# Gated cross-attention block on one core: inputs as one wide array, full-width fillers, rings of four, a new order

## The reference

```python
q  = layernorm(x);   qp = (q @ W1.T + b1) @ W2.T + b2;   kp = (ctx @ W1.T + b1) @ W2.T + b2
x  = x + tanh(g_xattn) * softmax(qp @ kp.T / sqrt(128) + mask) @ ctx
h  = relu(fixed_quant(quant(layernorm(x)) @ quant(w1).T + quant(b1)))      # 512 hidden features
x  = x + tanh(g_ffn) * (quant(h) @ quant(w2).T + quant(b2))
```

## Time and profile before

| what | value |
|---|---|
| runs of the kernel | 67.88, 69.7, 67.76 us |
| median | 67.88 us |
| profiled execution, span from first to last instruction | 68.7 us |
| the profiled execution's own time | not listed apart; its span lies 0.8 us above the median |
| busy: PE, DVE, ACT, POOL | 61.4, 54.9, 50.4, 48.1 us |
| instructions | 1887 |
| read from and written to memory | 6.75 MB, 2.10 MB |

### The profile page before, as it was taken

One profiled execution on the slowest core, in us unless ns is written; L12 is line 12 of the kernel. 1 busy time (PEld: TensorE's weight loads), 2 busy tenths in 40 slices (PEclk: granted clock), 3 DMA queues, 4 the chain that ended last, 5 costly groups with the idle time before them and its releaser, 6 DMA issues.

```text
span 68.7 us, 1887 instructions
## 1 busy us (share of the span) xinstructions
PE 61.4 (89%) x557; PEld 47.7 (69%) x557; DVE 54.9 (80%) x304; ACT 50.4 (73%) x137; POOL 48.1 (70%) x100
## 2 busy tenths in 40 slices
PE   4959999998999799898989999999999999998740
PEld 4939965783587559385956968897979778464520
DVE  4554814769819899999999999999999999896530
ACT  0710442898947966896999989999989979679610
POOL 5939075399995799967989999988999308770000
PEclk9999999999999999999999999999999999999999
DMA  0899999999999991000000002000304041242142
GB/s 0 243 280 337 261 381 266 310 252 294 310 225 297 248 206 36 0 14 0 5 0 5 0 2 74 10 0 20 132 0 153 16 152 47 106 153 100 53 157 76
DMA packets 5547, 8.96 MB, mean 131 GB/s; under 512 B 744, under 2 KB 2777, under 8 KB 5537
## 3 DMA queue, kind: packets, MB, share of 16 engines
q1 hardware_dynamic: 5247, 8.66, 42.8%
q10 hardware_dynamic: 290, 0.19, 0.9%
HBM read 6.75 MB, written 2.10 MB: 129 GB/s over the span
## 4 chain that ended last, share of the span: by engine, by line
PE 54%; DVE 17%; ACT 14%; DMA 5%; issue 5%; ACTq 1%; DVEq 0%
PE bank_A L460 9%; PE bank_T L422 8%; PE bank_S L444 8%; PE bank_O L501 7%; ACT pr L568 6%; DVE x_sb L671 5%; DMA ap_sb<-in_attn_par 5%; PE bank_H L486 5%; ACT h L595 4%; PE bank_H L388 4%; PE bank_A L453 4%; DVE st L612 3%; PE bank_T L435 3%; DVE h L698 3%; DVE y_sb L707 2%
## 5 line engine op out<-in xcount | busy, mean ns | idle before, releaser
L595 ACT ACTIVATE h<-bank_H,fb_q 128x512 int8<-128x512 f32 (+1 forms) x27 | 15.8, 642 | 2.3 <-PE bank_H L486 2.2
L612 DVE BATCH_NORM_STATS2 st<-x_sb 128x6 f32<-128x128 f32 x64 | 14.0, 277 | 1.4 <-DMA x_sb<-in_x 1.3
L356 POOL TENSOR_SCALAR xq<-x_sb,nm,rs 128x128 int8<-128x128 f32 x30 | 13.2, 458 | 0.5
L568 ACT ACTIVATE pr<-sc,mn 128x120 f32<-128x120 f32 x32 | 12.2, 384 | 1.8 <-DVE mn L659 1.8
L334 POOL TENSOR_TENSOR rs<-ve,half 128x4 f32<-128x4 f32 (+1 forms) x9 | 8.5, 945 | 7.0 <-DVE nm L619 7.0
L346 POOL TENSOR_SCALAR xn<-x_sb,nm,rs 128x128 f32<-128x128 f32 x28 | 12.3, 453 | 0.6
L338 POOL TENSOR_TENSOR rs<-ve,half 128x4 f32<-128x4 f32 (+1 forms) x9 | 8.5, 941 | 4.3 <-DVE nm L619 4.3
L659 DVE CUSTOM_DVE_ANT_0 sc<-bank_S,mask_neg 128x120 f32<-128x120 f32 x32 | 7.1, 273 | 3.9 <-PE bank_S L444 3.9
L671 DVE SCALAR_TENSOR_TENSOR x_sb<-bank_A,rec,x_sb 128x128 f32<-128x128 f32 x32 | 9.1, 341 | 1.1 <-DVE rec L664 0.9
L444 PE MATMUL bank_S<-kpT,xaT 128*128 128x120 f32 x64 | 9.4, 290 | 0.3 <-DVE mn L659 0.3
L444 PEld LDWEIGHTS bank_S<-kpT,xaT 128*128 128x128 f32 x64 | 8.4, 200 | 1.8 <-issue 1.5
(11 more groups left out here) (78 smaller groups left out, 99.2 us busy)
## 6 DMA issues: line engine op xcount, KB each, us to landing
x_sb<-in_x SPq DMA_DIRECT2D x7, 256.0 KB, 8.1
out_y<-y_sb SPq DMA_DIRECT2D x7, 256.0 KB, 2.0
kT_sb<-in_ctx_kT SPq DMA_DIRECT2D x7, 240.0 KB, 8.5
v_sb<-in_ctx_v SPq DMA_DIRECT2D x7, 240.0 KB, 9.5
mp_sb<-in_mlp_par SPq DMA_DIRECT2D x1, 514.0 KB, 6.5
x_sb<-in_x SPq DMA_DIRECT2D x2, 128.0 KB, 8.2
out_y<-y_sb SPq DMA_DIRECT2D x2, 128.0 KB, 1.7
kT_sb<-in_ctx_kT SPq DMA_DIRECT2D x2, 120.0 KB, 8.3
```

Source lines behind the costliest of these rows:

```text
L356: nc.gpsimd.tensor_scalar(low_byte(xq16[g % RING], tile(j)), x_sb[:, of(g, j)], nm2[:, of(g, j, 1)], rs2[:, of(g, j, 1)], ALU.add, ALU.mul ...
L568: nc.scalar.activation(pr[i][:, j, :], sc[i][:, j, :], ACT.Exp, scale=-1.0, bias=mn[:, of(g, j, 1)], accum_out=den[:, of(g, j, 1)]).then_i ...
L595: nc.scalar.activation(low_byte(h16[g % RING], hcols(c, g)), bank_H[c][:, cols(g)], ACT.Relu, bias=fb1_q[:, c:c + 1]).then_inc(h_act[c], 1)
L612: nc.vector.bn_stats(st[:, START[g] + j, :], x_sb[:, of(g, j)]).then_inc(st_done, 1)
```

## The change

All inputs but the row of gates lie in one array of 128 rows, "feed", whose columns stand in the order in which they are loaded; values (v) are padded from 120 to 128 rows. LOADS names fourteen transfers on SP and ACT's one ("a", the attention parameters): x0; k0 with the mask; x1; v0 with k1; x2 with v1; the weights "w"; then k(g), x(g+1), v(g) of a group as one transfer of 752 KB, k7 x8 v7 of 624 KB, and k8 v8. Each transfer has one semaphore, for which every reader of any of its parts waits. ACT no longer loads the mask.

Fillers are 128 columns wide instead of 64: 30 at the start, 12 after the first fold matmul, 3 before project_keys(0); the other packs are gone. RING is 4; one more of the large byte memsets runs on DVE (HBYTES_DVE = 2), as does the fourth xq16 one, and POOL keeps two. DUE now holds places in each engine's own order; who does which tile or chunk is as before, while the order differs on every engine. The core of the diff; the new places stand in full for the steps that the text speaks of:

```diff
-RING = 3
-
-
+RING = 4
 XN_ON_POOL = [2, 3, 4, 4, 4, 4, 3, 2, 2]
 XQ_ON_POOL = [2, 3, 4, 4, 4, 4, 4, 4, 1]
 RELU_ON_ACT = [3, 4, 3, 3, 2, 3, 3, 3, 3]
-
-
+HBYTES_DVE = 2
+LOADS = ['a', 'x0', 'k0 m', 'x1', 'v0 k1', 'x2 v1', 'w', 'k2 x3 v2', 'k3 x4 v3', 'k4 x5 v4', 'k5 x6 v5', 'k6 x7 v6',
+ 'k7 x8 v7', 'k8 v8']
+ACT_LOADS = [0]
+OPENING = 30
+FILLERS = [12, 3]
...
+    fold_mm1=[1],
+    fold_mm2=[2],
+    transpose_x=[3, 8, 14, 18, 24, 30, 41, 48, 61],
+    spread_gates=[4],
+    project_keys=[5, 6, 11, 15, 20, 27, 34, 44, 58],
+    scores=[7, 10, 17, 21, 28, 37, 45, 52, 63],
+    transpose_probs=[9, 16, 23, 29, 35, 43, 51, 57, 67],
+    attend=[12, 19, 26, 32, 38, 46, 54, 60, 69],
+    fold_base=[13],
+    transpose_xq=[22, 33, 39, 47, 53, 59, 64, 70, 73],
+    hidden=[25, 36, 42, 50, 56, 62, 66, 72, 75],
+    mlp_out=[31, 40, 49, 55, 65, 68, 71, 74, 76],
+    copy_xT=[1, 8, 12, 16, 22, 29, 40, 48, 60],
+    copy_keys=[2, 5, 11, 14, 19, 26, 32, 44, 58],
+    exponentials=[7, 13, 17, 25, 30, 39, 47, 54, 65],
+    copy_probsT=[9, 15, 21, 28, 33, 42, 50, 56, 68],
+    scale_weights=[10],
+    copy_xqT=[20, 31, 38, 46, 53, 57, 63, 70, 74],
+    stats1=[1, 3, 5, 9, 13, 15, 18, 33, 38],
+    fold_cp1=[2],
+    fold_cp2=[4],
+    row_maxima=[6, 10, 16, 19, 26, 34, 42, 48, 57],
+    normalise_dve=[0, 7, 0, 0, 0, 0, 30, 40, 0],
+    reciprocals=[8, 14, 20, 25, 32, 39, 47, 52, 61],
+    residual=[11, 17, 22, 28, 35, 43, 49, 55, 63],
+    stats2=[12, 21, 24, 31, 37, 45, 51, 58, 64],
+    relu_dve3=[23, 0, 41, 46, 53, 56, 60, 67, 69],
+    quantise_dve=[0, 27, 0, 0, 0, 0, 0, 0, 66],
+    result=[29, 36, 44, 50, 59, 62, 65, 68, 70],
+    rstd1=[1, 3, 5, 8, 11, 13, 19, 23, 29],
+    normalise_pool=[2, 4, 6, 9, 14, 16, 22, 26, 31],
+    widen_weights=[7],
+    rstd2=[10, 17, 20, 24, 27, 30, 33, 35, 37],
+    quantise_pool=[12, 18, 21, 25, 28, 32, 34, 36, 38],
+    split_base=[15],
+    keep_warm0=[1.5],
+    keep_warm1=[4.5],
...
+def block_of(name):
+    return name[0], int(name[1:] or 0)
+
+
+def flamingo_gated_block(nc, feed, rows, out, D, K, HID):
...
+        spans, place, at = {}, {}, 0
+        for n, names in enumerate(LOADS):
+            for name in names.split():
+                kind, g = block_of(name)
+                size = {"a": 2 * D + 2, "m": K, "w": C * (P + D + 1), "k": TILES[g] * K}.get(kind, TILES[g] * D)
+                spans[name], place[name] = (at, at + size), n
+                at += size
+
+        def fed(name, first=0, size=None):
+            lo, hi = spans[name]
+            return feed_sb[:, lo + first:(hi if size is None else lo + first + size)]
+
+        def x_of(g, j):
+            return fed(f"x{g}", j * D, D)
+
+        def v_of(g, j):
+            return fed(f"v{g}", j * D, D)[0:K, :]
+
+        ap_sb, mask_sb, mp_sb = fed("a"), fed("m"), fed("w")
         W2T_sb, W1b1_sb, b2_sb = ap_sb[:, 0:D], ap_sb[:, D:2 * D + 1], ap_sb[:, 2 * D + 1:2 * D + 2]
         tg = sb("tg", [P, 2])
         tg_out = sb("tg_out", [P, 1])
...
-        zeros_h = sb("zeros_h", [P, P // 2], BF16)
+        zeros_h = sb("zeros_h", [P, P], BF16)
...
+        load_in = [sem(f"load_in{n}") for n in range(len(LOADS))]
+        row_in, y_out = sem("row_in"), sem("y_out")
+
+        def wait_block(engine, name):
+            engine.wait_ge(load_in[place[name]], 16)
...
+        def load(engine, n):
+            names = LOADS[n].split()
+            part = slice(spans[names[0]][0], spans[names[-1]][1])
+            engine.dma_start(feed_sb[:, part], feed[:, part]).then_inc(load_in[n], 16)
...
+            for n, names in enumerate(LOADS):
+                if n not in ACT_LOADS:
+                    load(sp, n)
...
-            for i in range(1, RING):
+            for i in range(HBYTES_DVE, RING):
...
-                    nc.tensor.matmul(bank_H[3][0:P // 2, 0:P // 2], zeros_h[:, :], zeros_h[:, :], start=True, stop=True)
+                    nc.tensor.matmul(bank_H[3][:, 0:P], zeros_h[:, :], zeros_h[:, :], start=True, stop=True)
 
             pe.wait_ge(zeros_up, 1)
-            keep_warm(36)
+            keep_warm(OPENING)
...
-            act.dma_start(ap_sb[:, :], attn_par).then_inc(ap_in, 16)
+            for n in ACT_LOADS:
+                load(act, n)
             act.dma_start(row_sb[:, :], rows).then_inc(row_in, 16)
-            act.dma_start(mask_sb[:, :], mask).then_inc(mask_in, 16)
...
-            nc.vector.memset(h16[0][:, :].bitcast(F32), BYTE_PAIR).then_inc(bytes_up, 1)
+            for i in range(HBYTES_DVE):
+                nc.vector.memset(h16[i][:, :].bitcast(F32), BYTE_PAIR).then_inc(bytes_up, 1)
```

More of the change, by code:

```diff
@@ L34 @@
 RELU_ON_ACT = [3, 4, 3, 3, 2, 3, 3, 3, 3]
-DUE = dict(
[L39 to L90, removed]
@@ L100, in before @@
         return sum(self[:g])
[L103 to L107, removed]
+def block_of(name):
+    return name[0], int(name[1:] or 0)
+def flamingo_gated_block(nc, feed, rows, out, D, K, HID):
+    P = feed.shape[0]
+    B = sum(TILES)
     G = len(TILES)
@@ L110, in flamingo_gated_block @@
     TG = max(TILES)
-    C = mlp_par.shape[1] // (P + D)
+    C = HID // P
     N = TG * D
@@ L146, in flamingo_gated_block @@
         tg_out = sb("tg_out", [P, 1])
-        mp_8 = sb("mp_8", list(mlp_par.shape), I8)
+        mp_8 = sb("mp_8", [P, C * (P + D + 1)], I8)
         w1_q = sb("w1_q", [P, C * P], BF16)
@@ L534, in scale_weights @@
             def scale_weights():
-                act.wait_ge(mp_in, 16)
-                nc.scalar.activation(mp_8[:, :], mp_sb[:, :], ACT.Copy, scale=W_SCALE).then_inc(quant8, 1)
+                wait_block(act, "w")
+                nc.scalar.activation(mp_8[:, :], mp_sb, ACT.Copy, scale=W_SCALE).then_inc(quant8, 1)
                 act.wait_ge(row_in, 16)
@@ L726, with columns @@
     c = np.ascontiguousarray
[L727 to L736 removed]
+    START = [sum(TILES[:g]) for g in range(len(TILES) + 1)]
+    x_cols = c(a["x"].transpose(1, 0, 2).reshape(S, Bn * D))
+    kT_cols = c(a["ctx_1024"].transpose(2, 0, 1).reshape(D, Bn * S2))
+    v_cols = np.zeros((P, Bn * D), np.float32)
+    v_cols[:S2] = a["ctx_1024"].transpose(1, 0, 2).reshape(S2, Bn * D)
+    def columns(name):
+        kind, g = block_of(name)
+        if kind == "a":
+            return np.concatenate([a["L0_xattn_W2"].T, a["L0_xattn_W1"], a["L0_xattn_b1"].reshape(D, 1),
+                                   a["L0_xattn_b2"].reshape(D, 1)], axis=1)
+        if kind == "w":
+            return np.concatenate([a["L0_ffn_w1"].T,
+                                   a["L0_ffn_w2"].T.reshape(C, P, D).transpose(1, 0, 2).reshape(P, C * D),
+                                   a["L0_ffn_b1"].reshape(C, P).T], axis=1)
+        if kind == "m":
+            return a["fside_1xSxS2_0"].reshape(S, S2)
+        wide, n = {"x": (x_cols, D), "k": (kT_cols, S2), "v": (v_cols, D)}[kind]
+        return wide[:, START[g] * n:START[g + 1] * n]
+    arrays = {
+        "feed": c(np.concatenate([columns(name) for names in LOADS for name in names.split()], axis=1)),
         "rows": np.concatenate([a["g_xattn"].reshape(1, 1), a["g_ffn"].reshape(1, 1),
```

95 lines of the change are left out of this document (33 added, 62 removed).

## The result

| | kernel before | changed kernel |
|---|---|---|
| median, us | 67.97 (67.76 to 69.70, 4 runs) | 66.81 (66.70 to 68.71, 4 runs) |
| ratio | 1 | 0.983 (0.981 to 0.985) |
| profiled execution, span, us | 68.7 | 64.9 |

The ratio compares only executions that agree with the shortest of their kernel; the longer ones (69.7, 68.71) are left out of it, and what sets them apart turned out to be part of the answer.

A forecast was written before the change was run, and what follows sets the result against it. A head where DVE starves, a middle DVE bounds, a tail of dependences. 3.6 - 0.7 + 0.2 - 0.2 (fillers) = 2.9 us, 0.2 given back: 67.88 - 2.6 = 65.3 us, chance 0.60, range 64.0 to 66.4.

The forecast's parts named there:

- the last one of the sum: Base of the forecast: profiled span 0.8 above the median, so 0.2 us given back; 67.88 - 2.6 = 65.3 us.
- the largest term: Head, 4.08 to 20.30: DVE's idle time falls from 6.3 to 2.7 us, 3.6 us gained, bounds 2.2 and 4.3.
- fold_base: Step moved to PE's thirteenth place: PE stands from about 13.5 to 15.1; price on DVE 0, up to 1.5 us.
- Clock: PE in the head: full-width fillers bring the upper clock at 5 to 8 us instead of 12; up to 2.5 go.
- DVE in the head: New DVE order: row_maxima(0) at 10.3, stats1(3) at 12.6, stats2(0) ended by 16.6; 3.6 us of idle time gained.
- Middle and tail: Middle: 0.7 us more DVE waiting (bounds 0 and 2.5); tail after the last statistics: 0.2 gained (-1 to +1).
- Loads: Grouped transfers with 6016-byte rows: about 360 GB/s against 281; k2+x3+v2 lands at 12.1 to 13.4, taken as 12.6 us.
- Extra constants: Two more memsets on DVE, 1.18 us, fit into its 1.34 us wait for x0; four buffers alone taken as 0.
- rival 1: ACT and PE in the middle eat the head's gain: 3.6 less 2.5 waiting, 66.8 us; chance 0.13.
- rival 2: PE's clock in the head doesn't rise sooner; only loads and order help: gain 1.0, 66.9 us; chance 0.10.
- rival 4: Coarse load k2+x3+v2 comes later than 14 us, DVE queued behind stats1(3): 1.4 us of gain gone, 66.6; chance 0.08.
- Rival 3: PE's clock falls back at its fold_base stand, 13.5 to 15.1: 4 to 5.5 us slower, say 69.8; chance 0.09.

The follow-up runs named there:

- the second profile: The kernel before, unchanged, profiled anew: 68.11, 67.79, 69.99 and 67.95 us; the profile is of the execution with a span of 66.3 us.

## Why the prediction was right or wrong

**The step that failed is the last one of the sum.** It reads: "The profiled execution's own time isn't listed by itself; its span lies 0.8 above the median ... I give back 0.2 for that". A span was set beside times as if nothing lay between them. The runs show 1.8 us around nearly every span of the kernel before, so the profiled execution had taken about 70.5, 2.6 us above the median, not 0.8. Its surplus over the second profile, 2.4 us, was a late start of the loads (0.8) and the late clock (1.6), the very thing whose removal was part of the largest term. So 2.4 us, not 0.2, had to be given back: the executions with an early clock, which the ratio compares, had that part of the gain already. With 2.4 the prediction's own sum leaves 0.5 us, 67.4; the measured 1.2 is more than that. Two of the three times shown were below the profiled span; that alone should have stopped the sum. (There is a slip of 0.1 in it as well: 2.9 less 0.2 is 2.7, not 2.6.)

The signs that the prediction named for being right all came: score matmuls in 0.68 us, ending before 10; DVE idle 3.15 us, below 3.3; loads above 330 GB/s; fold_base at 14.13. They test the walk through the profile. None of them tests the base from which the gain is subtracted.

**Clock.** Right in kind, wrong in its base. Against the execution profiled first the upper clock came 8 us earlier and the doubled work went. But this is no privilege of the wide fillers: 64-column fillers also bring it by 6 us in some executions. The text said "without effect before 12 us"; that was one draw. In the old order the late draw is absent with wide packs (0 of 11 runs of two versions) and frequent with narrow ones (23 of 37 of the kernel before, by their times); whether by the width or because the wide pack lasts until the parameters have landed is open. The shortest executions don't change. The Trainium skill (TensorE: Matmul & The Clock Gate, Part 1: The HAM clock gate) says that the warm-up is run-variable, and these runs show it. It also puts the ramp penalty below 1% of a typical kernel's span; here a late rise cost 1.6 us in one profile and 2.5 in another, on a span of 66.3, which is 2.4 and 3.8%.

**DVE in the head.** The walk held closely. Forecast and measured: row_maxima(0) at 10.3 and 9.64, stats1(3) at 12.6 and 11.26, scores(0) ended by 9.7 and at 9.5, fold_base ended its wait at 15.1 and 14.13, exponentials(1) 16.1 and 15.83. Idle from 4.08 to 20.30 was forecast at 2.7 and is 3.15. Against an execution with an early clock and early loads that is 4.92 to 3.15, 1.8 us instead of 3.6.

**Middle and tail.** A charge of 0.7 against 0.40 measured (idle 0.64 to 1.04); a gain of 0.2 in the tail against 0.22 (7.65 - 5.52 = 2.13 to 6.21 - 4.30 = 1.91, up to the ends at 64.15 and 62.71). With 1.77 - 0.40 + 0.22 less 0.15 more busy time from 4.08 on the end moves by 1.4 us, as the two spans say.

**Loads.** Estimated 360 GB/s, measured 386 from 12.00 to 20.30 (417 up to 18, as the loads end before 20.30), with k2+x3+v2 at 11.2 instead of 12.6. The reason given, longer rows, is the smaller part: out of the wide array rows of 2 KB or less reach 386 up to 18 us as well. Nothing came of it in either case.

**Extra constants.** "1.18 fits into it" held for the execution profiled, in which x0 came at 4.08. In other executions it comes sooner: with rings of three DVE starts its statistics at 3.51, with the fourth members' memsets at 4.00. The 0.5 us shows in no time, 66.93 against 66.81.

**fold_base.** "Price on DVE 0, up to 1.5": between the two versions with more fillers the place costs 0.4 (shortest) to 0.9 us (median); without them the medians show no price. That it acts through exponentials(1), 0.45 us sooner, is argued and not shown.

**Rivals.** The times of rivals 1, 2 and 4 (66.8, 66.9, 66.6) all fit the result, and that is luck: by their signs none occurred. DVE was idle 1.04 us from 20.30 to 56.50, not over 2.5 (rival 1); the score matmuls took 0.17 us each, not 0.29 (rival 2); stats1(3) was released at 11.26, not after 14 (rival 4). Rival 2 is nearest in sense: relative to an execution with an early clock the clock rose hardly sooner, and what helped was the order. Rival 3, the fall back, exists: it is seen in the narrow-filler profile, at 7.4 to 10.6 us rather than at fold_base, for 1.7 us rather than 4, and the granted clock of the changed kernel's own long run, 0.974, suggests it there too.

## What to carry to other kernels

Put the profiled span next to the measured times first, and find from any second kernel what lies between a span and its time; if the profile is of a long execution, price a change against the others. Where a single core starts with fillers, look at the spread as well as at the shortest time, and see in the profile whether PE stands idle between the fillers and its first real work. When two profiles of one kernel differ, follow one step after another and note where the lag grows: here 0.8 us of it stood at the first matmul, before the clock could matter. Name signs for the base of a forecast too, and not only for its walk. A big change of several parts is best taken apart by giving the new kernel its old order, and the old kernel each new part; here one part in four did the work.

## What the runs showed of the hardware that was not expected

- The kernel before has two lengths, 67.7 to 68.3 and 69.6 to 71.3 us; two profiles of it, at 66.3 and 68.7, differ by PE's upper clock from about 6 and about 12 us on (1.6 us) and by when the first loads landed (0.8 us). PEclk reads 1.00 in both the earlier trace rows: the lower level ahead of the first rise shows only in durations (1.15 and 0.70 us for the same four matmuls), while a fall after it does show, as 0.50.
- Transfers out of one wide array ran at 386 (rows of 2 KB or less) and 417 GB/s (rows of 6 KB) from 12 to 18 us, against 273 out of separate arrays with rows of 2 KB or less. What differs between the first and the last is the distance from row to row (53,752 bytes against 16,384 and 15,360) and v's 128 rows for 120. Which of the two it is stays open; neither was run alone.
- In some runs (three with fold_base later, three with hardly any fillers) 2.3 to 2.5 us lay around the span instead of 1.8, and in all six with one transfer per block 2.0 to 2.1. What adds them is open.
